# A recommendation tower on one core: first ids ahead of the dense part, linear passes split 6 and 14, squares and output products moved back

## The reference

```python
e = stack([tbl_f[ids[:, f]] for f in 26], axis=1)            # 512 x 26 x 64
x = layer_norm(dense @ Wd.T, gd, bd)                         # 512 x 128
y = layer_norm(einsum('bnd,ed->bne', e, Ws), gs, bs)
y = einsum('bne,pn->bep', y, Wsi); y = layer_norm(y, gsi, bsi)
T = concatenate([x[:, None, :], swapaxes(y, 1, 2)], axis=1)  # 33 vectors of 128
Z = einsum('bnd,bmd->bnm', T, T)                             # inner products
out = layer_norm(Z[:, tril] @ Wl.T, gl, bl)[:, :384]         # 528 -> 512
h = concatenate([out, dense], axis=1)
h = relu(h @ W_top1 + b1); h = relu(h @ W_top2 + b2); y = h @ W_top3
```

## Time and profile before

| | us |
|---|---|
| Median of 3 runs | 299.44 (298.72 to 300.36) |
| The profiled execution | 297.24 |
| its span, first to last instruction | 295.4 |
| PE busy | 154.6 (52%) |
| DVE busy | 130.5 (44%) |
| ACT busy | 107.0 (36%) |
| POOL busy | 100.9 (34%) |

### The profile page before, as it was taken

One profiled execution on the slowest core, in us unless ns is written; L12 is line 12 of the kernel. 1 busy time (PEld: TensorE's weight loads), 2 busy tenths in 40 slices (PEclk: granted clock), 3 DMA queues, 4 the chain that ended last, 5 costly groups with the idle time before them and its releaser, 6 DMA issues.

```text
span 295.4 us, 4646 instructions
## 1 busy us (share of the span) xinstructions
PE 154.6 (52%) x1819; PEld 116.9 (40%) x1819; DVE 130.5 (44%) x296; ACT 107.0 (36%) x242; POOL 100.9 (34%) x111
## 2 busy tenths in 40 slices
PE   0736400026000400022069797769898998898797
PEld 0514300003000300002015485447776777776696
DVE  4852300000100600000065778458989789978533
ACT  2020100000100100000046766587777767776522
POOL 3777777777777777773000000000000000000100
PEclk9997765555755555555559967579999999999999
DMA  6352231111111111110000000200002000100000
GB/s 192 105 203 63 97 98 25 25 26 27 27 27 27 27 27 27 26 25 18 0 0 3 0 2 0 46 0 2 3 3 46 0 2 2 39 11 23 23 2 0
DMA packets 6259, 9.59 MB, mean 32 GB/s; under 512 B 2687, under 2 KB 3794, under 8 KB 6110
## 3 DMA queue, kind: packets, MB, share of 16 engines
q0 software_dynamic: 3392, 3.45, 6.0%
q1 hardware_dynamic: 2488, 5.08, 5.7%
q10 hardware_dynamic: 358, 0.77, 0.9%
HBM read 8.01 MB, written 0.00 MB: 27 GB/s over the span
## 4 chain that ended last, share of the span: by engine, by line
issue 43%; PE 31%; ACT 13%; DVE 8%; DMA 3%; SPq 1%; ACTq 0%; DVEq 0%
PE psB L307 7%; ACT Zs L595 6%; PE psU L295 4%; PE psG L280 3%; PE psW L338 3%; DVE B L768 2%; ACT U L561 2%; DMA small_sb<-in_small 2%; DVE qA L746 2%; DVE prod L739 2%; PE psH L443 2%; PE psZ L322 2%; ACT sdB L573 2%; PE psW L443 1%; PE psH L452 1%
## 5 line engine op out<-in xcount | busy, mean ns | idle before, releaser
L253 POOL DMA_INDIRECT g_sb<-in_table,row_id x104 | 99.4, 956 | 31.7 <-issue 31.4
L768 DVE TENSOR_TENSOR B<-psB,bias 128x512 f32<-128x512 f32 x32 | 20.8, 687 | 114.2 <-remote 47.5
L307 PE MATMUL psB<-U,ws_g 64*128 64x512 f32 x64 | 21.9, 765 | 63.5 <-issue 52.9
L210 POOL DMA_DIRECT2D Zt<-Zs x2 | 1.1, 552 | 141.4 <-ACT Zs L595 141.4
L295 PE MATMUL psU<-wsi_x,g_sb 128*128 128x192 f32 (+4 forms) x128 | 26.6, 362 | 34.6 <-issue 30.0
L295 PEld LDWEIGHTS psU<-wsi_x,g_sb 128*128 128x128 f32 x128 | 24.1, 232 | 39.4 <-issue 33.3
L595 ACT ACTIVATE Zs<-psZ 32x264 f32<-32x264 f32 x60 | 37.1, 618 | 1.3 <-PE psZ L322 0.2
L567 ACT ACTIVATE sqB<-B 128x512 f32<-128x512 f32 x32 | 19.7, 633 | 43.2 <-DVE B L768 43.2
L307 PEld LDWEIGHTS psB<-U,ws_g 64*128 64x128 f32 x64 | 5.6, 215 | 68.1 <-issue 53.7
L280 PEld LDWEIGHTS psG<-gram,sT 128*128 128x128 f32 x104 | 15.8, 230 | 32.3 <-issue 24.0
L280 PE MATMUL psG<-gram,sT 128*128 128x128 f32 x104 | 19.3, 334 | 17.6 <-issue 17.6
(11 more groups left out here) (132 smaller groups left out, 217.8 us busy)
## 6 DMA issues: line engine op xcount, KB each, us to landing
g_sb<-in_table,row_id POOLq DMA_INDIRECT x104
wl_sb<-in_wl SPq DMA_DIRECT2D x1, 1280.0 KB
w_sb<-in_w SPq DMA_DIRECT2D x2, 512.0 KB
w_sb<-in_w SPq DMA_DIRECT2D x1, 768.0 KB
small_sb<-in_small SPq DMA_DIRECT2D x1, 615.5 KB, 6.4
dense_sb<-in_dense ACTq DMA_DIRECT2D x1, 512.0 KB, 3.6
Zt<-Zs SPq DMA_DIRECT2D x3, 80.0 KB
Zt<-Zs SPq DMA_DIRECT2D x3, 70.0 KB
```

The lines of the kernel that those rows point to most:

```text
L253: pool.indirect_dma_start(g_sb[:, k, h * DSP:(h + 1) * DSP], None, table, bass.IndirectOffsetOnAxis(row_id[:, 2 * k + h:2 * k + h + 1], 0) ...
L307: pe.matmul(psB[h][:, :], ws_g[h * DSP:(h + 1) * DSP, :], U[h * DSP:(h + 1) * DSP, u % 2, :], start=True, stop=True).then_inc(B_done, 1)
L768: dve.tensor_tensor(B[:, h, :].rearrange("p (s j) -> p s j", j=PROJ), psB[h][:, :].rearrange("p (s j) -> p s j", j=PROJ), bias[:, :].rearr ...
```

## The change

Four things, in the order of the program.

1. **First ids.** The ids array is laid out so that the first ids are one run of 16 numbers per partition; SP loads them first, then `small`, then the other ids. ACT's queue waits for the first ids (`act.wait_ge(d_ids, 16)`) before it issues the dense input and what follows it.
2. **Linear passes.** `EARLY` is 6 in place of 12: six linear matmuls in steps 6, 10 and 14, fourteen in steps 7, 11 and 15.
3. **Outputs.** `output(b-1)` stands behind the inner products and ahead of `linear(b, 0, EARLY)`, writes into `psH` in place of `psW`, and so needs `h1_scaled`. The copy of its result stands later on DVE. The last one writes into `psB[0]`. `fills` is waited for up to 5.
4. **End.** `squares_w(2)` leaves step 15 and stands behind the last copies and ACT's two relay DMAs; `layer1(2)` goes ahead of `variance(2)` on PE; `zT` of that block is copied as soon as `psW` is done.

```diff
-EARLY, ALL = 12, FLIN // P * CW
+EARLY, ALL = 6, FLIN // P * CW
@@ SP and ACT, start
-            sp.dma_start(ids_sb[:, :, 0:FIRST_IDS], ids[:, :, 0:FIRST_IDS]).then_inc(d_ids, 16)
-            sp.dma_start(ids_sb[:, :, FIRST_IDS:], ids[:, :, FIRST_IDS:]).then_inc(d_more, 16)
+            sp.dma_start(ids_sb[:, 0:2 * FIRST_IDS], ids[:, 0:2 * FIRST_IDS]).then_inc(d_ids, 16)
             sp.dma_start(small_sb[:, :], small).then_inc(d_small, 16)
+            sp.dma_start(ids_sb[:, 2 * FIRST_IDS:], ids[:, 2 * FIRST_IDS:]).then_inc(d_more, 16)
+            act.wait_ge(d_ids, 16)
             act.dma_start(dense_sb[:, :, :], dense).then_inc(d_dense, 16)
@@ PE: linear, variance, layer1, output
                     if b:
-                        pe.wait_ge(y_copied, b)
+                        pe.wait_ge(h2_ready, b)
...
                 pe.wait_ge(h2_ready, b + 1)
+                pe.wait_ge(h1_scaled, b + 1)
                 for k in range(K2):
-                    mm = pe.matmul(psW[0:1, FOUT:FOUT + BS], w3_c[:, k:k + 1], h2T[:, k * BS:(k + 1) * BS],
+                    mm = pe.matmul(psH[0:1, FOUT:FOUT + BS], w3_c[:, k:k + 1], h2T[:, k * BS:(k + 1) * BS],
@@ PE: step
-                if late and j == 0 and b:
-                    output(b - 1)
                 project(t)
...
                 if late and j == 0:
+                    if b:
+                        output(b - 1)
                     linear(b, 0, EARLY)
...
             inner(UNITS - 1)
+            layer1(LAST - 1)
             variance(LAST - 1)
-            layer1(LAST - 1)
             last_block()
@@ ACT: step 15 and the end
                     if t == UNITS - 1:
                         keep_z(t - 1, 0)
                         deviation_b(t, 1)
-                        squares_w(b)
                     keep_z(t - 1, 1)
...
             for q in (1, 4):
                 relay(act, LAST, q, 1, 2, d_zt_act)
+            squares_w(LAST - 1)
             deviation_w(LAST - 1)
@@ DVE
-                dve.wait_ge(W_squared, b + 1)
+                dve.wait_ge(W_squared if b < LAST - 1 else W_done, b + 1)
...
-                if late and j == 0 and b:
-                    copy_y(b - 1)
                 add_b(t, 0)
                 add_b(t, 1)
                 if t + 1 < UNITS:
                     mult_a(t + 1)
                     sums_a(t + 1)
+                if late and j == 0 and b:
+                    copy_y(b - 1)
                 sums_b(t, 0)
```

More of the change, by code:

```diff
@@ L78, in sem @@
             return ctx.enter_context(nc.semaphore(name))
-        ids_sb = sb("ids_sb", [P, 2, 2 * ALL_SLOTS], I32)
+        ids_sb = sb("ids_sb", [P, 4 * ALL_SLOTS], I32)
+        first_ids = ids_sb[:, 0:2 * FIRST_IDS].rearrange("p (a n) -> p a n", a=2)
+        more_ids = ids_sb[:, 2 * FIRST_IDS:].rearrange("p (a n) -> p a n", a=2)
         row_id = sb("row_id", [P, 2 * ALL_SLOTS], I32)
@@ L229, in _ @@
                 if b == 0:
-                    sp.wait_ge(fills, 4)
+                    sp.wait_ge(fills, 5)
                 for q in range(7):
@@ L245, in _ @@
             pool.wait_ge(d_ids, 16)
-            pool.tensor_tensor(row_id[:, 0:FIRST_IDS], ids_sb[:, 0, 0:FIRST_IDS], ids_sb[:, 1, 0:FIRST_IDS],
+            pool.tensor_tensor(row_id[:, 0:FIRST_IDS], first_ids[:, 0, :], first_ids[:, 1, :],
                                ALU.add).then_inc(ids_added, 1)
@@ L347, in variance @@
                 elif b < LAST - 1:
-                    pe.wait_ge(h1_scaled, b)
+                    pe.wait_ge(y_copied, b)
                 else:
@@ L430, in last_block @@
                 output(LAST - 1)
+                pe.wait_ge(h1s_f[0], 1)
                 for k in range(K2):
                     pe.wait_ge(h2T_f[k], 1)
-                    mm = pe.matmul(psH[0:1, 0:BS], w3_c[:, k:k + 1], h2T_last[:, k * BS:(k + 1) * BS],
+                    mm = pe.matmul(psB[0][0:1, 0:BS], w3_c[:, k:k + 1], h2T_last[:, k * BS:(k + 1) * BS],
                                    start=(k == 0), stop=(k == K2 - 1))
@@ L590, in keep_z @@
                     if b == 0:
-                        act.wait_ge(fills, 4)
+                        act.wait_ge(fills, 5)
                     if b >= 2:
@@ L600, in squares_w @@
                     act.wait_ge(W_summed, b)
+                if b == LAST - 1:
+                    act.wait_ge(zT_ready, b + 1)
                 act.activation(z_sq[:, :], psW[:, :], ACT.Square).then_inc(W_squared, 1)
@@ L838, in last_block @@
                 dve.wait_ge(y_done, BLOCKS)
-                dve.tensor_copy(y_sb[:, LAST * BS:], psH[0:1, 0:BS]).then_inc(y_copied, 1)
+                dve.tensor_copy(y_sb[:, LAST * BS:], psB[0][0:1, 0:BS]).then_inc(y_copied, 1)
             def copy_y(b):
@@ L843, in copy_y @@
                 dve.tensor_copy(y_sb[:, b * BS:(b + 1) * BS],
-                                psW[0:1, FOUT:FOUT + BS]).then_inc(y_copied, 1)
+                                psH[0:1, FOUT:FOUT + BS]).then_inc(y_copied, 1)
             dve.memset(eps_c[:, :], EPS).then_inc(eps_ready, 1)
@@ L855, in _ @@
             dve.wait_ge(d_more, 16)
-            dve.tensor_tensor(row_id[:, FIRST_IDS:], ids_sb[:, 0, FIRST_IDS:], ids_sb[:, 1, FIRST_IDS:],
+            dve.tensor_tensor(row_id[:, FIRST_IDS:], more_ids[:, 0, :], more_ids[:, 1, :],
                               ALU.add).then_inc(more_added, 1)
@@ L1043 @@
         "table": np.concatenate(tables, axis=0),
-        "ids": np.stack([chunks(x["ids"]), chunks(np.broadcast_to(starts, (BATCH, NSP)))], axis=1),
+        "ids": np.concatenate([a[:, lo:hi] for lo, hi in ((0, FIRST_IDS), (FIRST_IDS, 2 * ALL_SLOTS))
+                               for a in (chunks(x["ids"]), chunks(np.broadcast_to(starts, (BATCH, NSP))))], axis=1),
         "small": np.concatenate([
```

## The result

The changed kernel takes 301.56 us (median of 20 runs, 297.9 to 304.52), the one before 298.61 in the same comparison. The ratio is 1.0082, with a 95% interval of 1.0051 to 1.0112: 1.5 to 3.3 us slower. The profiled execution of the changed kernel took 301.54 us, its span 299.7, against 297.24 and 295.4 before. Runs of either kernel spread over 5 us and more, and one run of the kernel before took 773.93 us, so one pair of profiles gives the sizes of steps, and only the ratio gives the size of the whole. A ratio in this document counts, of each kernel, only the runs within 1.5% of its fastest one, so it can differ from the ratio of the medians by about 1%.

The account below looks back on a forecast made before the run. It took a slow stretch to about 149, then a loop of PE, ACT and DVE, as bounds. Terms -0.8 + 2.9 + 0.44 + 0.95 = +3.5 on the median 299.44 gave 302.9 us, range 299.8 to 305.2.

Parts of the forecast that it names:

- Linear passes, +2.9 in steps 7 and 11: Six linear matmuls moved ahead of the inner products delay ACT's copies up to `U`: 1.45 us each in steps 7 and 11.
- Outputs, +0.44: Steps 10 and 14: moved output matmuls are free, DVE's copy costs 0.28, `project` gains about 0.06: +0.22 us each.
- The end, +0.95: Step 15 to `last_block`: later inner products cost 1.45 us, removing the squares gives part back, 0.95 us stays.
- near tie of variance and landing: Before `last_block`: `variance(2)` on PE ends at 281.3, level with the relays' landing at 281.4.
- The start, -0.8: First ids to last gather: earlier ids bring the gathers forward, between 0 and 1.5 us; 0.8 us gain taken.
- my bound of 1.5: POOL's first add of the ids: at best at 3.1 in place of 4.63, a gain of 1.5 us.
- the crawl's end: End, near 149, of the slow first stretch where PE's results come late; claimed to move earlier with the gathers, by 0.8 us.
- The memset: Rival, chance 0.12: POOL's add waited for DVE's memset of `Zt`, so early ids bring nothing: +4.3, 303.7 us.
- The riding passes: Rival, chance 0.15: ACT's copies in steps 7 and 11 start late without moving `U`: +0.6, 300.0 us.
- The losing start: Rival, chance 0.13: dense or the row constants land 1.5 us late, about +1.5 in place of -0.8: 305.2 us.
- The clock in steps 4 and 5: Rival, chance 0.10: PE keeps the upper clock there, saving about 2 us a step: -1.3, 298.1 us.

Follow-up runs that it names:

- both tests of it: Kernel before with POOL pausing after 26 gathers, 181.88 us; kernel before with PE's first instruction held until the last gather, 309.64 and 310.23 us.

## Why the prediction held, point by point

I had 302.9, +3.5, and slower with 0.72; measured are 301.56 and +2.5 by the ratio (1.5 to 3.3). What lengthens the steps came as forecast; the start did not.

- **Linear passes, +2.9 in steps 7 and 11: shown.** 1.33 each, 2.66 in all. The small rest is PE's own: twelve more rows take 3.22 - 1.88 = 1.34 us, where I had taken 1.47 from a row of 24. ACT's first copy stands 0.75 behind the start of the inner products, as before (0.76). The edit alone gave the same steps to 0.01, taking it back gave those of before, and step 6 gained 0.03, as good as nothing, as reckoned.
- **Outputs, +0.44: right in sign, too large.** Steps 10 and 14 are 0.12 longer together. That is a difference of two things: the linear matmuls that left gave back 0.08 and 0.09, which I had counted as 0, and the outputs cost 0.15 and 0.14. DVE's scaled rows come 2.25 us after its first product in place of 2.06, so its copy of 0.28 cost 0.19. As I had said, the matmuls are free where six linear ones left; with twelve the outputs cost 0.4 in each of these steps. So two parts of the change depend on each other.
- **The end, +0.95: 0.96.** Both halves of it were seen apart: 0.52 gained by taking the squares out of ACT's line, 1.48 lost to the linear passes (28.71 against 27.23). The near tie of variance and landing was real, as far as rows tell: 3.43 us after the copies, the distance of before, would be 284.75 (an estimate), and the variance matmuls let `last_block` go at 284.85.
- **The start, -0.8: not shown, and its working did not hold.** The ids gained 2.04, above my bound of 1.5, because I took the trip of a relay, 1.7, as the shortest possible and kept the issue at 0.70; the issue took 0.42 and the trip 1.43. Of that the last gather kept 1.6, and the crawl's end moved with it (149.01 in place of 151.10; the row at 148.96 that I took for its end was not the last late one). The next step failed: I took PE to be as far by then as before. An earlier gather stream also slows PE earlier: `xT` came 21 us later, and the third `U` 0.65 later, not 0.8 earlier. I had also counted the late dense input as 5 to 6 us ahead of its use; PE waited 2.06 for it. In the one pair of profiles the start lost 0.6 up to the seventh `U`; by the runs of the start alone it is -1.2 (-3.0 to +0.5) by the ratio and +1.2 by the medians.
- **Rivals.** The memset does not hold POOL: its add ran at 2.59, inside the memset's 2.43 to 4.62. By that the section "Who interferes with whom" of the Trainium skill's page "SBUF — State Buffer" agrees with the trace. The riding passes fall by steps 7 and 11. The losing start was half there: dense is now last, with a wait of 2.06 us on PE, and PE does go into the crawl behind; the loss of 1.5 us that I gave it isn't shown. The clock in steps 4 and 5 stayed as it was in the changed kernel's profile (10.36 and 11.28 us). It did rise in the three other kernels with the start part (9.6 to 9.9 and 9.9 to 10.2) and in neither without it, so that rival stays open: whether the start part raises the clock there, or luck does, one execution each can't tell.

The steps and the end give 2.66 + 0.12 + 0.96 = 3.7 us, the ratio 2.5 (1.5 to 3.3), the pair of profiles 4.3. So the start and the run's other differences would be -1.2 by the first and +0.6 by the second. The forecast of the whole was near because its largest terms, 2.9 and 0.95, were right; that the start's term didn't spoil it is luck.

## What to carry to other kernels

Before work is moved from one step of a pipelined loop to another, look at what stands directly behind it in each: six matmuls were nearly free at the end of a step, where PE would next wait for VectorE, and cost their full length ahead of the inner products, where ScalarE's whole line waited. Parts of a change share the same room, so each is to be priced with the others in place and without. And one recurring instruction per step is a ruler: where the granted clock was at its upper level, the steps that the edits leave alone agreed to 0.03 us on chips of the first kind, while whole runs scatter by 5. Where the clock fell it did not hold (step 6: 7.80 and 9.41). When two ways to average the same few runs disagree in sign, neither is a finding.

## What the runs showed of the hardware

The same kernel took 298 us on chips of one kind and 182 to 183 on three of another. In the first kind ACT and DVE read PE's results late while gathers are issued: `mix(1)` had eight rows of PE done by 101, and ACT got it at 129.35, 21.1 us after it was through with the result before, some 2.6 us for each of the eight rows. PE's granted clock was mostly 0.5, which alone doesn't explain it: in step 4, at the same level, eight such rows took 2.48 us in all. Holding PE back until the last gather, on a chip of the second kind, gives 309.64, only 11 us more than the 298 of the first kind; by that estimate across two chips, PE gets little done beside the gathers there. In the second ACT waits 1.73 us for PE at the first `U` (rows of the end alone), and the granted clock reads 9 in most slices. In the first kind the last late result was read 15.0 to 16.6 us after the last gather's issue in six executions, and the slowness began earlier where the gathers did. The cause is open: both tests of it, in three runs, met chips that don't have it. What the rows do show is that a change is to be read from steps that both kinds share; the price of the linear matmuls was 1.33 us a step on the first kind and 1.3 to 1.6 on the second.
